# First attention of a decoder layer: queries rotated before the scores, both maps' scores as 64x64 quarters

## Chip, cores and metric

The kernel runs on one core of one Trainium2 chip. The metric is the device time of one launch in microseconds, as the median of several runs. The engines are TensorE (PE, with its weight loads shown apart as PEld), VectorE (DVE), ScalarE (ACT), GpSimd (POOL) and SyncE (SP), which here only issues DMAs. Each engine works through its own list of instructions in order, and semaphores order the lists against each other.

## What is computed

A decoder layer over 16 sequences of 128 tokens with 256 features: a first (differential) attention, a cross attention and a mixture of experts, each behind a layer norm and with a residual. The change touches the first attention alone:

```python
q = _apply_rope(q, cos, sin)            # 16 heads of 128; t*cos + rotate_half(t)*sin
k = _apply_rope(k, cos, sin)            # 4 key heads, each shared by 4 query heads
q1, q2 = (q[..., :64], q[..., 64:])
k1, k2 = (k[..., :64], k[..., 64:])
s1 = einsum('bhqd,bhkd->bhqk', q1, k1) / 8
s2 = einsum('bhqd,bhkd->bhqk', q2, k2) / 8
a1, a2 = softmax(masked s1), softmax(masked s2)     # causal, window of 64
diff = relu(a1 - lam * a2)
diff = diff / (sum(diff) + 1e-06)
out = (diff @ v) @ Wo
```

## The kernel before, in words

**Tiling.** The first attention runs in four groups `g` of four query heads with one key head. In a group there are 16 units `u`, one per sequence. Four units make a chunk `c` of 512 tokens. While the units of one chunk run, the projections of the next chunk are made: six items, `k`, `q0` to `q3` and `v`. `A_ITEMS` gives their order, `A_SLOT` the unit `j = u % 4` and the slot `s` at which each is made. They all go through the one PSUM bank `PJ`, so an item is projected only once the one before it has been taken out. The very first chunk is projected ahead of the loop, over four banks (`A_START`, `A_TURNS`). So 15 chunks are prepared inside units; the last four units prepare none.

**Order inside a unit.** Each engine's list is written out by hand in `a_unit`:
- PE: slot 0, the scores of unit `u` (L669), the transposes of `u-2` (L683, L685), slot 1, the product with the values of `u-2` (L692), the output projection of `u-3` (L701).
- DVE: denominators of `u-2` (L1100, L1105), residual of `u-4` (L1110), for `u-1` the reciprocal of the second map's sums and the ratio (L1080, L1084), **slot 0**, rho (L1088), the low part of the output of `u-3` (L1140), the difference of the maps of `u-1` (L1094), the row maxima of `u` (L1148, L1149), **slot 1**.
- ACT: slot 0 (the values' copy for item `v`), the copy of the transposes (`pt`, L1423), relu of `u-1` (L1500), the exponentials of `u` (L1456), slot 1, the copy `oah`, the mask written into the score banks for `u+2`.
- POOL: the normalisation of `u-2` (L1687), at `j = 0` the addition for the next chunk's keys (L1681), in the last chunk of a group the low parts of the next weights (L1675).

**Rotation.** In `a_take` DVE takes a query item out of PSUM with two multiplications of 128x512 (L1054): one product with (cos, -sin) for map 0, one with (sin, cos) for map 1, each over 128 rows. A key item costs three (L1044, L1046, the two of L1046 crossing between the halves of the partitions). POOL adds the key's two products, and four DMAs of 64 rows copy the rotated keys so that each map has its 64 key rows twice. The scores then contract over all 128 rows, and that contraction adds the two products of the query. One unit has 16 score products (2 maps, early and late query half, 4 heads), each with 64 columns of weights, so heads alternate between two column halves of the array. The trace shows each as two matmul records.

**Slots before.** `k` in (0, 1), `q0` in (1, 0), `q1` in (1, 1), `q2` in (2, 1), `v` in (3, 0), `q3` in (3, 1). On DVE, therefore, of the query and key items only `q0` stands in a slot 0.

Of the kernel before, what the change touches and what calls it, by code (L numbers as in the profile page):

```python
# [18 lines left out]
CB = 4  # L19
NC = B // CB  # L20
# [86 lines left out]
def decoder_kernel(nc, x, ctx_in, in_wqk, in_wv, in_wo, in_lam, in_taba, in_rawb, in_tabb, in_kvtab,  # L107
# [5 lines left out]
    def sem(name):  # L113
        return ctx.enter_context(nc.semaphore(name))
# [4 lines left out]
    with ctx:  # L119
# [111 lines left out]
        def quads(ap):  # L231
            return ap.rearrange("p (h k) -> p h k", k=S)
# [13 lines left out]
        a_hi, a_lo = sem("a_w_high"), sem("a_w_low")  # L246
        a_vf = sem("a_values_taken")
        a_pj, a_pf, a_k = sem("a_projected"), sem("a_projection_taken"), sem("a_k_ready")
        a_kd, a_tn = sem("a_k_copied"), sem("a_table_negated")
        a_sc, a_mx, a_ex = sem("a_scores"), sem("a_negmax"), sem("a_exp")  # L250
        a_mk = sem("a_mask_in_place")
        a_r2, a_rt, a_rh = sem("a_rec2"), sem("a_ratio"), sem("a_rho")
# [30 lines left out]

        A_ITEMS = ["k", "q0", "q1", "q2", "v", "q3"]
        AN, AV = len(A_ITEMS), A_ITEMS.index("v")
        A_SLOT = {(0, 1): 0, (1, 0): 1, (1, 1): 2, (2, 1): 3, (3, 0): 4, (3, 1): 5}
        AW = AN - 1


# [149 lines left out]
        def _(sp):  # L441
            for c in range(NC):
                if c == 0:
                    sp.dma_start(idf[:, :], ident).then_inc(s_const, 16)
                sp.dma_start(x_sb[:, CB * c:CB * (c + 1), :],
                             x[CB * c:CB * (c + 1)].rearrange("b p d -> p b d")).then_inc(s_x[c], 16)
                if c == 0:
                    sp.dma_start(raw_a[:, :, :], in_wqk[0]).then_inc(a_raw, 16)
                if c == 1:
                    sp.dma_start(taba[:, :, :], in_taba).then_inc(a_tab, 16)  # L450
                    for at in (0, QH):
                        sp.dma_start(maskf[at:at + QH, 0:QH], mask[0:QH, 0:QH]).then_inc(s_mask, 16)
                        sp.dma_start(masku[at:at + QH, :], mask[QH:S, :]).then_inc(s_mask, 16)
                    sp.dma_start(wv[:, :, :], in_wv).then_inc(a_wvl, 16)
            sp.dma_start(nlam[:, :], in_lam).then_inc(a_wld, 16)
            sp.dma_start(wo[:, :, :], in_wo).then_inc(a_wld, 16)
            for g in range(NG):
                if g < NG - 1:
                    sp.wait_ge(a_lo, g * AW + AW)
                    sp.dma_start(raw_a[:, :, :], in_wqk[g + 1]).then_inc(a_raw, 16)  # L460
                for c in range(NC):
                    sp.wait_ge(a_k, g * NC + c + 1)
                    for m in range(2):
                        for at in (0, 64):
                            sp.dma_start(kva[at:at + 64, c % 2, m, :], ktmp[64 * m:64 * m + 64, 0, :]).then_inc(a_kd, 16)
            sp.wait_ge(a_woh, NG)
            sp.wait_ge(a_wol, NG)
            sp.dma_start(raw_b[:, :], in_rawb[0]).then_inc(b_raw_s, 16)
# [78 lines left out]
        def _(pe):  # L547
# [69 lines left out]
            def a_unit(g, u, first=False, final=False, drain=False):  # L617
# [37 lines left out]
                if not drain:  # L655
                    if j == 0:
                        pe.wait_ge(a_pf, (g * NC + (c + 1)) * AW)
                        pe.wait_ge(a_vf, g * NC + (c + 1))
                        pe.wait_ge(a_kd, 64 * (g * NC + (c + 1)))
                    wait(pe, a_mk, n - 1)  # L660
                    tok = slice(S * j, S * (j + 1))
                    for m in range(2):
                        sc = A_S[u % 2][:, m, 0:SW]
                        if first and u < 2:
                            pe.matmul(sc, idb[:, :], maskb[:, :], start=True, stop=False, skip_group_check=True)
                        for at, to, keys in ((QH, late(sc), S), (0, early(sc), QH)):
                            for h in range(HG):
                                rows = slice(QH * (h % 2), QH * (h % 2) + QH)
                                last = pe.matmul(to[rows, h // 2, :],  # L669
                                                 qab[:, c % 2, m, h, S * j + at:S * j + at + QH],  # L670
                                                 kva[:, c % 2, m, S * j:S * j + keys],
                                                 start=False, stop=at == 0, skip_group_check=True)
                    last.then_inc(a_sc, 1)
                two = not (first and u < 2) and not (drain and u >= 2)
                if two:
# [219 lines left out]
            for c in range(len(A_START)):  # L895
# [4 lines left out]
                for item in A_START[c]:  # L900
                    if item == AV:
                        pe.wait_ge(a_wvl, 16)
                    a_project(0, 0, item, True, A_TURNS)
            pe.wait_ge(a_vf, 1)
            pe.wait_ge(s_cst, 3)
            pe.wait_ge(a_wld, 32)
            for u in range(UN):
# [79 lines left out]
        def _(dve):  # L987
# [47 lines left out]
            def a_take(g_to, c, item, turns=1):  # L1035

                chunk = g_to * NC + c
                if item == AV:
                    return
                dve.wait_ge(a_pj, chunk * AN + (item + 1))  # L1040
                src, par = quads(bank(PJ - (item % turns if turns > 1 else 0))), c % 2
                if item == 0:
                    wait(dve, a_kd, 64 * chunk)
                    dve.tensor_tensor(quads(ktmp[:, 0, :]), src, bcast(taba[:, 4, :]), ALU.mult)  # L1044
                    for to_, at in ((64, 0), (0, 64)):
                        last = dve.tensor_tensor(quads(ktmp[to_:to_ + 64, 1, :]), src[at:at + 64],  # L1046
                                                 taba[at:at + 64, 3, :].unsqueeze(1).broadcast_to([64, CB, S]),
                                                 ALU.mult)
                    last.then_inc(a_pf, 1)
                    return  # L1050
                h = a_tile(item) - 1
                to = ((qab[:, par, 0, h, :], 0), (qab[:, par, 1, h, :], 1))
                for dst, tab in to:
                    last = dve.tensor_tensor(quads(dst), src, bcast(taba[:, tab, :]), ALU.mult)  # L1054
                last.then_inc(a_pf, 1)

            def kv_step(i):
# [266 lines left out]
            ln_norm(0)  # L1324
            ln_stats(1)
            ln_low(0)
            dve.wait_ge(a_tab, 16)
            ln_norm(1)
            dve.wait_ge(s_const, 16)
            dve.wait_ge(s_mask, 64)  # L1330
# [1 line left out]
            dve.tensor_copy(early(maskb[:, :]), maskf[:, 0:QH].unsqueeze(1).broadcast_to([128, XP, QH]))\  # L1332
               .then_inc(s_cst, 1)
            dve.tensor_copy(late(maskb[:, :]), masku.unsqueeze(1).broadcast_to([128, XP, S])).then_inc(s_cst, 1)
            dve.tensor_scalar(taba[64:128, 0, :], taba[64:128, 0, :], -1.0, None, ALU.mult).then_inc(a_tn, 1)
            dve.tensor_scalar(taba[:, 3, :], taba[:, 3, :], -1.0, None, ALU.mult).then_inc(a_tn, 1)
            dve.wait_ge(a_tn, 2)
            for item in A_START[0]:
# [82 lines left out]
        def _(act):  # L1421
# [38 lines left out]
            def a_unit(g, u, first=False, final=False, drain=False):  # L1460
                n, c, j = g * UN + u, u // CB, u % CB

                def slot(s):
                    item = A_SLOT.get((j, s))
                    if item is None or drain or (final and c == NC - 1):
                        pass
                    elif item == AV:
                        a_take_v(g + 1 if c == NC - 1 else g, (c + 1) % NC)
                    elif c == NC - 2 and not final:
                        act.wait_ge(a_pj, (g * NC + (NC - 1)) * AN + (item + 1))  # L1470
                        a_high(g + 1, a_tile(item))
                    for what in A_EXTRA.get((a_part(first, final, drain), u, s), []):
                        if what[0] == "ln":
                            ln_take(what[1], what[2], PJ)
                        elif what[0] == "prep":
                            b_take(0, 0, what, what[1], None, bank(PJ))
                        elif what[0] == "kt2":
                            r = what[1]
                            act.wait_ge(b_kvp, r + 1)
                            if r == 0:  # L1480
                                act.wait_ge(a_sc, NG * UN - CB)
                            copy(kt2[:, CB * r:CB * (r + 1), :], quads(bank(PJ))).then_inc(b_kvc, 1)
                if u == 3 and not drain:
                    if first:
# [169 lines left out]
        def _(pool):  # L1654
# [23 lines left out]
            def a_keys(g_to, c):  # L1678

                pool.wait_ge(a_pf, (g_to * NC + c) * AW + 1)  # L1680
                pool.tensor_tensor(ktmp[:, 0, :], ktmp[:, 0, :], ktmp[:, 1, :], ALU.add).then_inc(a_k, 1)  # L1681

            def a_norm(n, par):

# [12 lines left out]
            def a_unit(g, u, first=False, final=False, drain=False):  # L1697
# [16 lines left out]
                    ln_rstd(6)  # L1714
                if drain:
                    return
                if final and c >= NC - 2:
                    if u == UN - 2 * CB:
                        a_keys(g, NC - 1)
                    return  # L1720
                if j == 0:
                    a_keys(g + 1 if c == NC - 1 else g, (c + 1) % NC)
                if 0 < u - CB * (NC - 2) <= CB:
                    for s in range(2):
                        item = A_SLOT.get(((u - 1) % CB, s), AV)
                        if item != AV:
                            a_low(g + 1, a_tile(item))
# [15 lines left out]
                a_low(0, tile)  # L1743
            a_keys(0, 0)
            ln_low(1)
            ln_rstd(2)
            ln_rstd(3)
            for u in range(UN):
# [211 lines left out]
```

## Time and profile before

| | us |
|---|---|
| median of 3 runs | 1334.43 (1333.85 to 1336.25) |
| the profiled execution | 1336.08 |
| its span in the trace | 1334.2 |
| busy PE / DVE / ACT / POOL | 1262.3 / 837.2 / 720.2 / 467.6 |
| mean granted PE clock | 0.986 of 2.4 GHz |

The first attention fills the span from about 28 to 480 us, the cross attention up to about 890, the experts the rest. A row of the trace has a start in us from the span's beginning, a duration, and in brackets the idle time just ahead of it with what ended it. Busy time tells how much an engine had to do, not who set the pace: for that one reads who waited for whom, unit by unit.

### The profile page before, as it was taken

The numbers are of one execution on the slowest core, as the hardware profiler recorded it, in microseconds if no ns is written. First come the engines' busy times: TensorE is split into PE (matmuls) and PEld (weight loads), VectorE is DVE, ScalarE is ACT, GpSimd is POOL, SyncE is SP. The second block draws the span as 40 slices with busy tenths as digits, with TensorE's granted clock in tenths as the row PEclk, the third lists the DMA queues.
The fourth block names the chain that finished last, engine by engine and source line by source line (L and its number), as shares of the span: only waits on it lengthen the run. The fifth ranks groups of instructions, "written<-read, shape, count | busy, mean of one in ns | idle before, by whom it ended". The sixth has DMA issues, their size and how long they took to land.

```text
span 1334.2 us, 27286 instructions
## 1 busy us (share of the span) xinstructions
PE 1262.3 (95%) x9584; PEld 993.9 (74%) x9584; DVE 837.2 (63%) x1986; ACT 720.2 (54%) x2746; POOL 467.6 (35%) x451
## 2 busy tenths in 40 slices
PE   5799999999999787999999999989999999999998
PEld 4678888888887564666666666657888888888887
DVE  6788888888888676566666656775443443434433
ACT  2788888888887753444444444464232332423322
POOL 3122113212211124445444544641152353533532
PEclk9899999999999989999999999999899999999999
DMA  6002000200012101111202101200324341144340
GB/s 222 17 18 57 18 17 18 57 17 17 17 34 92 31 16 48 60 33 58 67 17 92 33 17 33 76 1 1 111 67 139 68 126 52 39 139 77 57 93 31
DMA packets 34737, 72.78 MB, mean 55 GB/s; under 512 B 7872, under 2 KB 12992, under 8 KB 33344
## 3 DMA queue, kind: packets, MB, share of 16 engines
q1 hardware_dynamic: 34624, 71.32, 20.2%
q8 instruction: 66, 1.08, 0.3%
q14 instruction: 47, 0.39, 0.1%
HBM read 52.29 MB, written 2.23 MB: 41 GB/s over the span
## 4 chain that ended last, share of the span: by engine, by line
PE 74%; DVE 9%; ACT 8%; issue 4%; POOL 2%; DMA 1%; SPq 1%; DVEq 0%; POOLq 0%; ACTq 0%
PE ps L553 33%; PE ps L945 9%; PE ps L669 5%; PE ps L701 4%; PE ps L738 3%; PE ps L832 3%; ACT ea L1456 3%; PE ps L692 3%; PE ps L842 2%; PE ps L814 2%; PE ps L822 2%; PE ps L608 2%; ACT ea L1500 2%; DVE ea L1094 1%; PE ps L683 1%
## 5 line engine op out<-in xcount | busy, mean ns | idle before, releaser
L1828 POOL TENSOR_TENSOR sg<-sg,cw 128x512 f32<-128x512 f32 x88 | 113.6, 1291 | 260.4 <-ACT sg L1619 257.0
L1397 DVE TENSOR_TENSOR hh<-ps,sg 128x512 f32<-128x512 f32 x100 | 69.1, 691 | 179.1 <-POOL sg L1828 161.4
L1423 ACT ACTIVATE hhh<-hh 128x512 fp32r<-128x512 f32 x100 | 63.2, 632 | 213.8 <-DVE hh L1397 211.6
L1456 ACT ACTIVATE ea<-ps,negmax 128x64 f32<-128x64 f32 (+1 forms) x512 | 165.1, 342 | 6.7 <-DVE negmax L1149 6.7
L1423 ACT ACTIVATE pt<-ps 128x512 f32<-128x512 f32 x128 | 77.1, 602 | 169.7 <-PE ps L822 112.2
L1196 DVE TENSOR_TENSOR qcs<-ps,tabb 128x512 f32<-128x512 f32 x192 | 123.5, 686 | 64.8 <-PE ps L553 64.4
L553 PE MATMUL ps<-xnh,wch 128*128 128x512 f32 x400 | 157.3, 393 | 0.0
L553 PE MATMUL ps<-xnl,wch 128*128 128x512 f32 x400 | 157.1, 393 | 0.0
L553 PE MATMUL ps<-xnh,wcl 128*128 128x512 f32 x400 | 155.7, 389 | 0.0
L1687 POOL TENSOR_TENSOR ea<-ea,rden 128x128 f32<-128x128 f32 (+1 forms) x128 | 62.2, 506 | 263.1 <-DVE rden L1105 263.1
L1694 POOL TENSOR_TENSOR eb<-eb,rsum 128x512 f32<-128x512 f32 x64 | 67.4, 1054 | 180.2 <-DVE rsum L1240 180.0
L945 PE MATMUL ps<-wch,hhh 128*128 128x256 f32 x400 | 115.8, 290 | 4.2 <-DVE hhl L1399 2.4
L1399 DVE TENSOR_TENSOR hhl<-hh,hhh 128x512 fp32r<-128x512 f32 x100 | 75.5, 755 | 69.8 <-ACT hhh L1423 69.8
L945 PE MATMUL ps<-wch,hhl 128*128 128x256 f32 x400 | 113.6, 284 | 0.0
L945 PE MATMUL ps<-wcl,hhh 128*128 128x256 f32 x400 | 113.6, 284 | 0.0
L1456 ACT ACTIVATION_READ_ACCUMULATOR ea<-ps,negmax 128x1 f32 x512 | 107.3, 210 | 0.0
L1456 ACT ACTIVATE eb<-ps,negmax 128x128 f32<-128x128 f32 x256 | 90.7, 369 | 26.0 <-DVE negmax L1234 25.7
L669 PEld LDWEIGHTS ps<-kva,qab 128*64 128x64 f32 x2048 | 93.8, 140 | 13.2 <-issue 8.1
L669 PE MATMUL ps<-kva,qab 128*64 128x128 f32 (+1 forms) x2048 | 103.0, 254 | 0.0
L1619 ACT ACTIVATE sg<-ps 128x512 f32<-128x512 f32 x100 | 59.8, 598 | 71.9 <-PE ps L553 71.2
L701 PE MATMUL ps<-woh,oah 128*128 128x256 f32 x256 | 97.5, 381 | 0.7 <-DVE oal L1140 0.7
L1054 DVE TENSOR_TENSOR qab<-ps,taba 128x512 f32<-128x512 f32 x128 | 82.1, 683 | 19.5 <-PE ps L553 19.0
(154 smaller groups left out, 3307.3 us busy)
## 6 DMA issues: line engine op xcount, KB each, us to landing
raw_w<-in_rawb_dram SPq DMA_DIRECT2D x4, 2432.0 KB, 8.9
kva<-ktmp SPq DMA_DIRECT2D x64, 128.0 KB, 2.3
kvt<-qcs SPq DMA_DIRECT2D x64, 128.0 KB, 2.3
cw<-comb_d SPq DMA_DIRECT2D x32, 256.0 KB, 5.0
raw_w<-in_rawc_dram SPq DMA_DIRECT2D x4, 1920.0 KB, 8.4
cw<-comb_d SPq DMA_DIRECT2D x16, 224.0 KB, 4.8
raw_a<-in_wqk_dram SPq DMA_DIRECT2D x4, 768.0 KB, 5.8
cw<-comb_d SPq DMA_DIRECT2D x16, 192.0 KB, 5.8
```

Source lines behind the costliest of these rows:

```text
L553: last = pe.matmul(out_ap, w, m, start=n == 0, stop=n == len(steps) - 1)
L669: last = pe.matmul(to[rows, h // 2, :], qab[:, c % 2, m, h, S * j + at:S * j + at + QH], kva[:, c % 2, m, S * j:S * j + keys], start=False ...
L701: last = pe.matmul(ps[:, YB, 0:DM], o_[:, (u - 3) % 2, h, :], w_[:, h, :], start=h == 0 and i == 0, stop=h == HG - 1 and i == 2)
L945: last = pe.matmul(ps[:, j // 2, DM * (j % 2):DM * (j % 2 + 1)], h_[:, par, S * j:S * (j + 1)], w_[:, t, 2 * KT * 128:RC_T], start=begin a ...
L1054: last = dve.tensor_tensor(quads(dst), src, bcast(taba[:, tab, :]), ALU.mult)
L1196: last = dve.tensor_tensor(quads(qcs[:, b_at(t), m, :]), quads(bk), bcast(tabb[:, b_table(t), m, :]), ALU.mult)
L1397: dve.tensor_tensor(hh[:, par, :], bank(C_U[par]), sg[:, par, :], ALU.mult).then_inc(c_h, 1)
L1399: dve.tensor_tensor(hhl[:, par, :], hh[:, par, :], hhh[:, par, :].bitcast(f32), ALU.subtract)\
L1423: return act.activation(dst, src, ACT.Copy)
L1456: last = act.activation(dst(m, h), src, ACT.Exp, bias=negmax[:, par, i:i + 1], accum_out=sums[:, par, i:i + 1])
L1694: pool.tensor_tensor(src[:, par, :, :], src[:, par, :, :], rec[:, par, :].unsqueeze(2).broadcast_to([128, HG, S]), ALU.mult).then_inc(done, 1)
L1828: pool.tensor_tensor(sg[:, par, :], sg[:, par, :], cw[:, c % 2, t, :], ALU.mult).then_inc(c_hs, 1)
```

## The change

Queries are now rotated completely before the scores. DVE still makes two products per query item, one with cos in place and one with sin. SP sends the sine product across the two halves of the partitions with two DMAs of 64 rows into the other parity's buffer, and POOL adds it to the cosine product, one 128x512 addition per head (`a_queries`). The keys are added by POOL straight into `kva`; their four DMAs are gone. A map's score now contracts over 64 rows only: map 0 over partitions 0 to 63, map 1 over 64 to 127, so 16 products per unit run as 64x64 quarters, in an order that changes the quarter each time. The item order becomes `k, q0, q1, q2, q3, v`, in the slots (0, 0), (0, 1), (1, 0), (1, 1), (2, 0), (3, 0). For the first chunk DVE writes the sine products crossed by itself, in two halves per head. Table loads become four DMAs.

```diff
-        A_ITEMS = ["k", "q0", "q1", "q2", "v", "q3"]
+        A_ITEMS = ["k", "q0", "q1", "q2", "q3", "v"]
-        A_SLOT = {(0, 1): 0, (1, 0): 1, (1, 1): 2, (2, 1): 3, (3, 0): 4, (3, 1): 5}
+        A_SLOT = {(0, 0): 0, (0, 1): 1, (1, 0): 2, (1, 1): 3, (2, 0): 4, (3, 0): 5}
...
-                    sp.dma_start(taba[:, :, :], in_taba).then_inc(a_tab, 16)
+                    sp.dma_start(taba[0:64, :, :], in_taba[0:64]).then_inc(a_tab, 16)
+                    sp.dma_start(taba[64:128, 0, :], in_taba[64:128, 1]).then_inc(a_tab, 16)
+                    sp.dma_start(taba[64:128, 1, :], in_taba[64:128, 0]).then_inc(a_tab, 16)
+                    sp.dma_start(taba[64:128, 2:6, :], in_taba[64:128, 2:6]).then_inc(a_tab, 16)
...
-                    sp.wait_ge(a_k, g * NC + c + 1)
-                    for m in range(2):
-                        for at in (0, 64):
-                            sp.dma_start(kva[at:at + 64, c % 2, m, :], ktmp[64 * m:64 * m + 64, 0, :]).then_inc(a_kd, 16)
+                    for h in range(HG if g or c else 0):
+                        sp.wait_ge(a_pf, (g * NC + c) * AW + (h + 2))
+                        for to, at in ((64, 0), (0, 64)):
+                            sp.dma_start(qab[to:to + 64, 1 - c % 2, 1, h, :], qab[at:at + 64, c % 2, 1, h, :])\
+                              .then_inc(a_qx[h], 16)
...
-                        pe.wait_ge(a_kd, 64 * (g * NC + (c + 1)))
+                        pe.wait_ge(a_k, g * NC + (c + 1))
+                        pe.wait_ge(a_qr, HG * (g * NC + (c + 1)))
...
+                    for at, part, keys in ((QH, late, S), (0, early, QH)):
+                        for m, h in ((0, 0), (1, 1), (0, 1), (1, 0), (0, 2), (1, 3), (0, 3), (1, 2)):
+                            rows, d = slice(QH * (h % 2), QH * (h % 2) + QH), slice(64 * m, 64 * m + 64)
+                            last = pe.matmul(part(A_S[u % 2][:, m, 0:SW])[rows, h // 2, :],
+                                             qab[d, c % 2, 0, h, S * j + at:S * j + at + QH],
+                                             kva[d, c % 2, 0, S * j:S * j + keys],
+                                             start=False, stop=at == 0, skip_group_check=True)
...
-                to = ((qab[:, par, 0, h, :], 0), (qab[:, par, 1, h, :], 1))
-                for dst, tab in to:
-                    last = dve.tensor_tensor(quads(dst), src, bcast(taba[:, tab, :]), ALU.mult)
+                dve.tensor_tensor(quads(qab[:, par, 0, h, :]), src, bcast(taba[:, 0, :]), ALU.mult)
+                if turns == 1:
+                    last = dve.tensor_tensor(quads(qab[:, par, 1, h, :]), src, bcast(taba[:, 1, :]), ALU.mult)
+                else:
+                    for to_, at in ((64, 0), (0, 64)):
+                        last = dve.tensor_tensor(quads(qab[to_:to_ + 64, 1 - par, 1, h, :]), src[at:at + 64],
+                                                 taba[at:at + 64, 1, :].unsqueeze(1).broadcast_to([64, CB, S]),
+                                                 ALU.mult)
...
-                pool.tensor_tensor(ktmp[:, 0, :], ktmp[:, 0, :], ktmp[:, 1, :], ALU.add).then_inc(a_k, 1)
+                pool.tensor_tensor(kva[:, c % 2, 0, :], ktmp[:, 0, :], ktmp[:, 1, :], ALU.add).then_inc(a_k, 1)
+
+            def a_queries(g_to, c, heads):
+
+                for h in heads:
+                    if isinstance(g_to, int) and g_to == 0 and c == 0:
+                        pool.wait_ge(a_pf, h + 2)
+                    else:
+                        pool.wait_ge(a_qx[h], 32 * (g_to * NC + c))
+                    q = qab[:, c % 2, 0, h, :]
+                    pool.tensor_tensor(q, q, qab[:, 1 - c % 2, 1, h, :], ALU.add).then_inc(a_qr, 1)
+
+            A_TURNED = [(), (0,), (1, 2), (3,)]
...
                 if j == 0:
                     a_keys(g + 1 if c == NC - 1 else g, (c + 1) % NC)
+                a_queries(g + 1 if c == NC - 1 else g, (c + 1) % NC, A_TURNED[j])
...
             a_keys(0, 0)
             ln_low(1)
+            a_queries(0, 0, range(HG))
```

## Rows read from the trace of the kernel before

**Rows 1.** The page: busy time of each engine, share of the span.

```profile
PE 1262.3 (95%) x9584; PEld 993.9 (74%) x9584; DVE 837.2 (63%) x1986; ACT 720.2 (54%) x2746; POOL 467.6 (35%) x451
PE 74%; DVE 9%; ACT 8%; issue 4%; POOL 2%; DMA 1%; SPq 1%; DVEq 0%; POOLq 0%; ACTq 0%
```

**Rows 2.** Windows view, one chunk's four units: busy time of each engine.

```profile
299.23:326.08 26.85, 26.75 (x250) 22.21 (x249) 22.08 (x64) 23.42 (x113) 7.24 (x12) 1.00 0.09 21
```

**Rows 3.** Timeline of DVE in that chunk: start, duration, instruction.

```profile
299.23 0.18 DVE L1080 RECIPROCAL rec<-sums 128x4 f32<-128x4 f32 x1 [0.72 <-ACT ea L1456]
...
306.19 0.18 DVE L1080 RECIPROCAL rec<-sums 128x4 f32<-128x4 f32 x1 [0.19 <-ACT ea L1456]
...
307.29 0.99 DVE L1094 SCALAR_TENSOR_TENSOR ea<-ea,rho 128x64 f32<-128x64 f32 x4
...
309.13 0.68 DVE L1044 TENSOR_TENSOR ktmp<-ps,taba 128x512 f32<-128x512 f32 x1
309.82 1.39 DVE L1046 TENSOR_TENSOR ktmp<-ps,taba 64x512 f32<-64x512 f32 x2
...
312.09 0.18 DVE L1080 RECIPROCAL rec<-sums 128x4 f32<-128x4 f32 x1
...
312.96 1.29 DVE L1054 TENSOR_TENSOR qab<-ps,taba 128x512 f32<-128x512 f32 x2 [0.36 <-PE ps L553]
314.17 0.15 DVE L1088 TENSOR_TENSOR rho<-ratio,a_gap 128x4 f32<-128x4 f32 x1
...
319.65 0.18 DVE L1080 RECIPROCAL rec<-sums 128x4 f32<-128x4 f32 x1 [0.55 <-ACT ea L1456]
...
320.06 0.69 DVE L1088 TENSOR_TENSOR rho<-ratio,a_gap 128x4 f32<-128x4 f32 x1
```

**Rows 4.** Timeline of ACT in that chunk.

```profile
301.92 0.60 ACT L1423 ACTIVATE pt<-ps 128x512 f32<-128x512 f32 x1 [1.01 <-PE ps L685]
...
308.31 0.26 ACT L1500 ACTIVATE ea<-ea 128x64 f32<-128x64 f32 x1
...
309.39 0.30 ACT L1456 ACTIVATE ea<-ps,negmax 128x64 f32<-128x64 f32 x1
```

**Rows 5.** Chain that ended last, scores of a unit in either attention: start, time.

```profile
305.54 1.49 PE ps L669 x32
...
601.14 0.60 PE ps L814 x16
```

**Rows 6.** Timeline of POOL in that chunk.

```profile
311.29 1.29 POOL L1681 TENSOR_TENSOR ktmp<-ktmp 128x512 f32<-128x512 f32 x1 [5.37 <-DVE ktmp L1046]
...
319.25 1.48 POOL L1675 TENSOR_TENSOR wal<-raw_a,wah 128x256 fp32r<-128x256 f32 x2
```

**Rows 7.** Timeline of DVE at 422 us.

```profile
422.24 1.19 DVE L1094 SCALAR_TENSOR_TENSOR ea<-ea,rho 128x64 f32<-128x64 f32 x4
```

**Rows 8.** Timeline of POOL at 422 us.

```profile
421.65 0.97 POOL L1687 TENSOR_TENSOR ea<-ea,rden 128x128 f32<-128x128 f32 x2
```

**Rows 9.** Chain, crossing of the second attention's products: the later of four issues, then landing.

```profile
521.18 1.84 SPq L488
...
523.06 2.33 DMA kvt<-qcs
```

**Rows 10.** Timeline of PE: projections at full clock, then after an idle time.

```profile
312.07 0.40 PE L553 MATMUL ps<-xnh,wah 128*128 128x512 f32 x1
...
422.68 0.41 PE L683 MATMUL ps<-idf,ea 128*64 128x128 f32 x2 [2.17 <-POOL ea L1687]
...
423.66 0.63 PE L553 MATMUL ps<-xnl,wah 128*128 128x512 f32 x1
```

**Rows 11.** Chain: projection of the values of the first and the fourteenth prepared chunk.

```profile
54.55 1.80 PE ps L608 x16
...
404.14 1.79 PE ps L608 x16
```

**Rows 12.** Chain: the first unit's start.

```profile
29.14 0.32 PE ps L665
```

More of the change, by code:

```diff
@@ L248, in decoder_kernel @@
         a_pj, a_pf, a_k = sem("a_projected"), sem("a_projection_taken"), sem("a_k_ready")
-        a_kd, a_tn = sem("a_k_copied"), sem("a_table_negated")
+        a_qx = [sem(f"a_q_sines_crossed{h}") for h in range(HG)]
+        a_qr, a_tn = sem("a_q_rotated"), sem("a_table_negated")
         a_sc, a_mx, a_ex = sem("a_scores"), sem("a_negmax"), sem("a_exp")
@@ L658, in a_unit @@
                         pe.wait_ge(a_vf, g * NC + (c + 1))
-                        pe.wait_ge(a_kd, 64 * (g * NC + (c + 1)))
+                        pe.wait_ge(a_k, g * NC + (c + 1))
+                        pe.wait_ge(a_qr, HG * (g * NC + (c + 1)))
                     wait(pe, a_mk, n - 1)
                     tok = slice(S * j, S * (j + 1))
[L662 to L672, printed above, removed]
+                    if first and u < 2:
+                        for m in range(2):
+                            pe.matmul(A_S[u % 2][:, m, 0:SW], idb[:, :], maskb[:, :], start=True, stop=False,
+                                      skip_group_check=True)
+                    for at, part, keys in ((QH, late, S), (0, early, QH)):
[5 more added lines that the diff above has]
+                                             start=False, stop=at == 0, skip_group_check=True)
                     last.then_inc(a_sc, 1)
@@ L904, in _ @@
             pe.wait_ge(a_vf, 1)
+            pe.wait_ge(a_pf, AW)
             pe.wait_ge(s_cst, 3)
@@ L1042, in a_take @@
                 if item == 0:
-                    wait(dve, a_kd, 64 * chunk)
+                    wait(dve, a_k, chunk)
                     dve.tensor_tensor(quads(ktmp[:, 0, :]), src, bcast(taba[:, 4, :]), ALU.mult)
@@ L1326, in _ @@
             ln_low(0)
-            dve.wait_ge(a_tab, 16)
+            dve.wait_ge(a_tab, 64)
             ln_norm(1)
@@ L1334, in _ @@
             dve.tensor_copy(late(maskb[:, :]), masku.unsqueeze(1).broadcast_to([128, XP, S])).then_inc(s_cst, 1)
-            dve.tensor_scalar(taba[64:128, 0, :], taba[64:128, 0, :], -1.0, None, ALU.mult).then_inc(a_tn, 1)
+            dve.tensor_scalar(taba[64:128, 1, :], taba[64:128, 1, :], -1.0, None, ALU.mult).then_inc(a_tn, 1)
             dve.tensor_scalar(taba[:, 3, :], taba[:, 3, :], -1.0, None, ALU.mult).then_inc(a_tn, 1)
@@ L1480, in slot @@
                             if r == 0:
-                                act.wait_ge(a_sc, NG * UN - CB)
+                                act.wait_ge(a_sc, NG * UN - CB + 1)
                             copy(kt2[:, CB * r:CB * (r + 1), :], quads(bank(PJ))).then_inc(b_kvc, 1)
@@ L1716, in a_unit @@
                     return
-                if final and c >= NC - 2:
-                    if u == UN - 2 * CB:
-                        a_keys(g, NC - 1)
+                if final and c == NC - 1:
                     return
@@ L1722, in a_unit @@
                     a_keys(g + 1 if c == NC - 1 else g, (c + 1) % NC)
+                a_queries(g + 1 if c == NC - 1 else g, (c + 1) % NC, A_TURNED[j])
+                if final:
+                    return
                 if 0 < u - CB * (NC - 2) <= CB:
```

## Prediction

> **What bounds the kernel now.** The page comes first: PE is busy 95% of the span and makes up 74% of the chain that ended last [rows 1]. That invites the reading that every microsecond taken from PE is a microsecond won. The windows view of one chunk seems to agree: PE 26.75 of 26.85 us, ACT 23.4, DVE 22.1, POOL 7.2 [rows 2]. But a busy PE may be one that just keeps up, so I went on to the timelines of DVE and ACT in that chunk, and followed one closed loop through a unit. It starts when DVE takes the reciprocal of the second map's sums (L1080), which needs the exponentials of unit u-1. Then come ratio, whatever stands in slot 0, rho, the output's low part and the difference (L1094); then ACT's relu, which stands ahead of the exponentials in ACT's list; then the exponentials of unit u; then DVE's next L1080. In the unit that starts at 306.19, the difference begins 1.10 us after L1080 [rows 3], relu 2.12 us and the exponentials 3.20 us after it [rows 4], and the next L1080 stands at 312.09, 5.90 us later [rows 3]. PE has no part in this loop. DVE's rows in the same unit show the three key products, 2.08 us from 309.13 on, lying beside the exponentials, in slot 1, for nothing.
>
> The four windows from L1080 to L1080 are now readable. Unit j = 3, from 299.23: 6.96 us, because ACT's copy of the transposes waited 1.01 us for PE and relu stands behind it [rows 4]; this one is PE's. Unit j = 0: 5.90, the bare loop. Unit j = 1, from 312.09: 7.56; here `q0` stands in slot 0, DVE waited 0.36 us for its projection and needed 1.21 us from 312.96 to rho at 314.17. Unit j = 2, from 319.65: 6.43, the bare loop and 0.53 us in rho [rows 3], of which below. The sum is 26.85. So PE and the loop are both near the limit, but PE sets the time in one unit of four.
>
> **The change, part by part.**
>
> *Scores.* 32 records take 1.49 us per unit now. The nearest row for 64x64 quarters is the second attention's: 16 records in 0.60 us [rows 5], so 32 would take 1.20 us if each costs the same. Half of the records are only half as long, which gives at best 0.75 times this, 0.90 us. I take 1.05: 0.44 us less per unit, 1.8 us per chunk, 28 us over 64 units if PE were the bound. It isn't one afterwards (below), so what it buys is the PE wait of unit j = 3: its window goes from 6.96 to 5.90.
>
> *Slots.* DVE's work per item stays as it is: two products for a query, three for keys. But `k` moves from slot 1 to slot 0 of j = 0, `q1` takes the slot 0 of j = 1, where `q0` stood, and `q3` moves into slot 0 of j = 2. Slot 1 lies beside the exponentials, slot 0 lies in the loop. The windows become: j = 0, 5.90 + 2.08 = 7.98; j = 1, 5.90 + 1.21 = 7.11; j = 2, 7.11; j = 3, with `v` alone, which ACT takes out, 5.90. The sum is 28.1 us, 1.3 more than the 26.85 of before, although PE and DVE have no more to do than then. This is a floor: no part of the loop gets shorter.
>
> *POOL's additions.* `k` still costs one, and four queries are added: 4 x 1.29 us per chunk, by the same shape [rows 6]. POOL has the time (7.2 of 26.85 us busy), so as engine time they cost nothing. What they cost is DVE's. While a POOL operation runs, a DVE instruction that reads both inputs from SBUF does not start: rho, 0.15 us otherwise, took 0.69 from 320.06 to 320.75 [rows 3], just when POOL's 1.48 us from 319.25 ended [rows 6]; the difference at 422.24 took 1.19 in place of 0.99 [rows 7], POOL being busy till 422.62 [rows 8]. Products out of PSUM don't wait. The Trainium skill has this as a rule (page SBUF — State Buffer, section Who interferes with whom): a DVE instruction with two SBUF inputs and a GpSimd one that reads SBUF exclude each other, for the whole instruction. By that rule, the trace agrees, and without it this part would be free.
>
> Where do the additions fall? `k`: POOL starts when its products are done, at 2.5 us of window j = 0, and ends at 3.8. Rho slips in ahead, the 0.6 us low part reads PSUM, the difference would begin at 3.18 and waits till 3.86: 0.7 us. `q0`: its sine product is done at about 6.9 of window j = 0 (slot 1), the crossing costs two issues and a landing, bounded by the second attention's 1.84 + 2.33 = 4.2 us [rows 9] and by 1.2 + 2.33, so the addition starts at 1.7 to 2.4 of window j = 1, again against rho and the difference: 0.7. `q1`: its crossing is early, but POOL does the normalisation first (about 6.5 to 7.4), so the addition runs over the start of window j = 2 and holds ratio: 0.7. `q2` lands at 1.6 to 2.4 of window j = 2, right behind: 0.6. `q3` ends about with window j = 2, for nothing. Bounds of each: 0 and 1.29. I take 2.7 us per chunk, since each place follows from the order of the lists and not from chance: 30.8 us. The normalisation itself is not late, for it precedes the additions in POOL's list.
>
> *SP and DMA.* The wait for the key's copies goes; eight small DMAs per chunk come in place of four. The scores of the next chunk wait for `q3`'s addition, which ends before window j = 3 begins, one window ahead. The load of the second attention's first weights now stands behind the last crossing in SP's list, some two windows later than before, and is used only in the chunk after: no cost, or under 1 us once. DMA is busy 9% [rows 2].
>
> *Start.* The scores of unit 0 began at 29.14 [rows 12], behind `q3`'s products. Now DVE needs three products in place of two for each of four heads (2.7 us more), and POOL makes its four additions only behind its low part, the last some 1.3 us behind `q3`. The scores start about 3.4 us later; some of it returns, as `k` of the next chunk is then already projected. 2.5 us, between 0 and 4.
>
> *End.* The last four units prepare nothing and have shorter scores: 0 to 2 us gained, I take 2.
>
> **The sum.** Before, 14 prepared chunks are 13 intervals from 54.55 to 404.14 [rows 11], 26.9 us each. Afterwards 30.8: 3.9 more for 13 chunks, 50.7. The first two run beside layer norms, which fill part of DVE's list there already: 2.5 more each (between 1.3 and 3.9), 5. With the start 2.5 and the end -2: 56 us. The profiled execution took 1336.1 us for a span of 1334.2; it becomes 1392. The median of before is 1.7 us lower, so I forecast **1390 us**. PE then has about 24.3 us of work in 30.8.
>
> The Trainium skill (page TensorEngine Tiling (Array Packing), section PSUM Bottleneck) warns that after a TensorE speed-up by tiling, the emptying of PSUM may become the bottleneck. The rows say it already is half of the bound here: the loop consists of DVE and ACT instructions alone.
>
> **The rivals.**
>
> *A, the forecast:* the loop carries two more items and the additions. 1390. Chance 0.60.
>
> *B, the additions find gaps.* If most of them start beside instructions that read PSUM, the chunk is 28.1 to 29: 15 x 1.3 to 15 x 2.1 is 20 to 32 us, 1355 to 1366. For it: the row maxima, the products and the low part read PSUM and together fill over a third of a window. Against it: the places worked out above. 0.17.
>
> *C, the clock falls too.* With the loop as bound PE idles. At the start of window j = 3 it has done everything up to the transposes and waits for ACT's copy, by my count up to 3 us. Before, after 2.17 us idle, projections took 0.63 us in place of 0.40 [rows 10]: the 1.2 GHz level in place of 2.4. Then the output projection and `k`'s projection behind it take 1.3 us longer, and DVE waits for `k` at the slot 0 of j = 0. At up to 1.3 us for most chunks: 8 to 20 us on A, 1398 to 1410. 0.15.
>
> *D, PE was the bound (faster).* If slot 0's items found room in waits of DVE that I took for loop, the 0.44 us per unit come back: 1334 - 27 is 1307, with the start 1310. This decides if the bare loop is under 5.90 - 0.8 us, so that 4 windows with 4.5 us of items fit into 25 us. Rows 3 and 4 show no idle time of that size in it. 0.06.
>
> *E, the quarters don't overlap.* If products in different quarters run no faster than now, PE has 26.1 us of work per chunk, still under 28.1: the time is A's or B's. As a case of its own with no change in time: 0.02.
>
> **How the numbers follow.** The range takes in B's low end and most of C: 1354 to 1405. A measurement of this kernel can tell about 0.2%, 2.7 us, from no change. Faster by more 0.06, within 0.02, slower 0.92.
>
> **What would show it.** DVE's rows per chunk: windows of about 8.7, 7.8, 8.4 and 5.9 us; L1044 and its followers between ratio and rho; rho or difference lengthened, each ending with a POOL addition. ACT waiting for DVE's difference as its largest wait. PE busy about 80% in 160 to 480 us and waiting for DVE's takes. 32 score records in 0.9 to 1.2 us. The second attention and the experts as long as before. I am wrong if the chunk comes below 28 us, if windows with an item in slot 0 are 5.9 us, or if rho and difference keep their durations next to POOL's additions.

## Result and profile after

The changed kernel takes **1400.65 us** (median of 4 runs, 1396.79 to 1409.33), the kernel before 1334.3 us (1333.85 to 1336.25): slower by 5.0%, ratio 1.050 with a 95% interval of 1.0477 to 1.0524. The forecast was 1390, range 1354 to 1405. The profiled execution took 1396.8 us with a span of 1395.0, so the traces have 60.8 us between them to explain.

The page of the changed kernel: busy time, then the chain by engine, then ACT's relu and POOL's query additions (busy, mean ns, idle before and what ended it).

```profile
PE 1249.3 (90%) x9584; PEld 956.7 (69%) x9584; DVE 867.2 (62%) x1990; ACT 721.3 (52%) x2746; POOL 550.3 (39%) x515
PE 58%; DVE 17%; ACT 15%; issue 7%; POOL 2%; DMA 1%; SPq 0%; DVEq 0%; POOLq 0%; ACTq 0%
...
L1512 ACT ACTIVATE ea<-ea 128x64 f32<-128x64 f32 (+1 forms) x256 | 69.2, 273 | 96.5 <-DVE ea L1106 96.5
L1703 POOL TENSOR_TENSOR qab<-qab 128x512 f32<-128x512 f32 x64 | 83.2, 1303 | 36.5 <-DMA qab<-qab 36.5
```

Beside [rows 1] PE has fallen from 74% to 58% of the chain, DVE has gone from 9 to 17 and ACT from 8 to 15. POOL's 64 query additions are new, 83.2 us. Ahead of its relu (now L1512) ACT stood idle for 96.5 us waiting for DVE's difference (now L1106), before for 19.1: that is the loop, seen from ACT.

One undisturbed chunk, windows view (time, then busy PE, PEld, DVE, ACT, POOL, granted clock, DMA share, GB/s), to be put beside [rows 2]:

```profile
256.00:286.26 30.26, 24.58 (x246) 18.98 (x238) 23.50 (x63) 22.52 (x110) 10.29 (x13) 1.00 0.16 36
```

PE now works 24.6 of 30.3 us, at full clock. Timeline of DVE in that chunk, lines that answer to [rows 3]: L1092 (was L1080) opens each window, L1096 is the ratio, L1100 rho, L1106 the difference, L1051 and L1053 take the keys, L1059 and L1061 a query.

```profile
256.00 0.18 DVE L1092 RECIPROCAL rec<-sums 128x4 f32<-128x4 f32 x1 [1.08 <-ACT ea L1468]
...
256.40 0.69 DVE L1051 TENSOR_TENSOR ktmp<-ps,taba 128x512 f32<-128x512 f32 x1
257.11 1.39 DVE L1053 TENSOR_TENSOR ktmp<-ps,taba 64x512 f32<-64x512 f32 x2
258.53 0.16 DVE L1100 TENSOR_TENSOR rho<-ratio,a_gap 128x4 f32<-128x4 f32 x1
...
259.34 1.34 DVE L1106 SCALAR_TENSOR_TENSOR ea<-ea,rho 128x64 f32<-128x64 f32 x4
...
264.49 0.18 DVE L1092 RECIPROCAL rec<-sums 128x4 f32<-128x4 f32 x1 [1.09 <-ACT ea L1468]
...
266.68 2.03 DVE L1106 SCALAR_TENSOR_TENSOR ea<-ea,rho 128x64 f32<-128x64 f32 x4
...
272.51 0.18 DVE L1092 RECIPROCAL rec<-sums 128x4 f32<-128x4 f32 x1 [1.09 <-ACT ea L1468]
272.73 0.69 DVE L1096 TENSOR_TENSOR ratio<-rec,sums 128x4 f32<-128x4 f32 x1
...
274.54 0.50 DVE L1100 TENSOR_TENSOR rho<-ratio,a_gap 128x4 f32<-128x4 f32 x1
...
280.36 0.18 DVE L1092 RECIPROCAL rec<-sums 128x4 f32<-128x4 f32 x1 [1.59 <-ACT ea L1468]
...
286.26 0.18 DVE L1092 RECIPROCAL rec<-sums 128x4 f32<-128x4 f32 x1 [0.67 <-ACT ea L1468]
```

The windows are 8.49, 8.02, 7.85 and 5.90 us. The last one, with nothing of DVE's in slot 0, is the bare loop of before to a hundredth. And POOL in the same stretch, to be laid beside DVE's lengthened lines:

```profile
258.58 1.29 POOL L1693 TENSOR_TENSOR kva<-ktmp 128x512 f32<-128x512 f32 x1 [3.72 <-DVE ktmp L1053]
...
266.73 1.37 POOL L1703 TENSOR_TENSOR qab<-qab 128x512 f32<-128x512 f32 x1 [2.59 <-DMA qab<-qab]
...
272.12 1.28 POOL L1703 TENSOR_TENSOR qab<-qab 128x512 f32<-128x512 f32 x1
273.75 1.27 POOL L1703 TENSOR_TENSOR qab<-qab 128x512 f32<-128x512 f32 x1 [0.35 <-DMA qab<-qab]
```

Each addition holds up a VectorE instruction with two inputs in SBUF (this exclusion is "the port" below): POOL's 258.58 to 259.87 meets the difference at 259.34 (1.34 in place of 1.00); 266.73 to 268.10 meets it at 266.68 (2.03); the ratio at 272.73 ends at 273.42, with the addition that ended at 273.40; rho at 274.54 ends at 275.04, with the one from 273.75 on, which ended at 275.02.

**Where the 60.8 us are.** Counting from L1080 or L1092 of one chunk to that of the next:

| stretch | before | after | difference |
|---|---|---|---|
| first L1080/L1092 at | 39.89 | 42.02 | 2.1 |
| first 13 chunks | 351.9 | 407.0 | 55.1 (4.24 each) |
| next two | 66.1 | 69.7 | 3.6 |
| last units, nothing prepared | 28.2 | 25.9 | -2.3 |
| second attention, experts | | | 2.3 |

The undisturbed chunk gives 3.9 (30.26 against 26.4 in the best chunks of before). Most of the rest of the 4.24 is in window j = 3 of three chunks, one in each group behind the first: 7.02, 6.77 and 6.78 us instead of 5.90. There ACT converts the group's output weights (1.09 us) just ahead of the values and the copy of the transposes. Before, that window was PE's, 6.99 with this conversion against 6.96 without, so the conversion cost nothing; now it costs 0.9 to 1.1.

### The profile page after: what moved, and what is told of

Same layout as the page of the kernel before. It is cut to its first block, busy times and chain, and to the rows that moved or that the text cites. A ratio compares the mean times of both kernels' runs of the same rounds, so it can differ in the third digit from the quotient of the medians.

```text
span 1395.0 us, 27420 instructions
## 1 busy us (share of the span) xinstructions
PE 1249.3 (90%) x9584; PEld 956.7 (69%) x9584; DVE 867.2 (62%) x1990; ACT 721.3 (52%) x2746; POOL 550.3 (39%) x515
## 4 chain that ended last, share of the span: by engine, by line
PE 58%; DVE 17%; ACT 15%; issue 7%; POOL 2%; DMA 1%; SPq 0%; DVEq 0%; POOLq 0%; ACTq 0%
PE ps L558 27%; PE ps L952 9%; ACT ea L1468 8%; DVE ea L1106 4%; ACT ea L1512 3%; PE ps L744 3%; PE ps L838 3%; PE ps L848 2%; PE ps L820 2%; PE ps L828 2%; PE ps L707 2%; PE ps L698 2%; DVE ktmp L1053 2%; DVE qab L1061 1%; DVE rho L1100 1%
## 5 line engine op out<-in xcount | busy, mean ns | idle before, releaser
L1512 ACT ACTIVATE ea<-ea 128x64 f32<-128x64 f32 (+1 forms) x256 | 69.2, 273 | 96.5 <-DVE ea L1106 96.5
L698 PE MATMUL ps<-pt,kva 128*128 128x512 f32 x128 | 74.8, 668 | 42.3 <-DVE oal L1152 24.6
L558 PE MATMUL ps<-xnh,wah 128*128 128x512 f32 x160 | 71.1, 445 | 41.2 <-DVE qab L1061 21.7
L707 PE MATMUL ps<-woh,oah 128*128 128x256 f32 x256 | 100.7, 393 | 0.7 <-DVE oal L1152 0.7
L1703 POOL TENSOR_TENSOR qab<-qab 128x512 f32<-128x512 f32 x64 | 83.2, 1303 | 36.5 <-DMA qab<-qab 36.5
```

The lines of the kernel that those rows point to most:

```text
L558: last = pe.matmul(out_ap, w, m, start=n == 0, stop=n == len(steps) - 1)
L698: pe.matmul(bank(OB), quads(kva[:, (w // CB) % 2, 2, :])[:, w % CB, :], pt[:, u % 2, :, :], start=True, stop=True).then_inc(a_pv, 1)
L707: last = pe.matmul(ps[:, YB, 0:DM], o_[:, (u - 3) % 2, h, :], w_[:, h, :], start=h == 0 and i == 0, stop=h == HG - 1 and i == 2)
L1512: last = act.activation(e, e, ACT.Relu, accum_out=rsum[:, par, h:h + 1])
L1703: pool.tensor_tensor(q, q, qab[:, 1 - c % 2, 1, h, :], ALU.add).then_inc(a_qr, 1)
```

## Experiments

The kernel before was run beside each; its median lay between 1334.3 and 1336.1.

**Old scores, new slots.** The kernel before with the item order and slots alone:

```diff
-        A_ITEMS = ["k", "q0", "q1", "q2", "v", "q3"]
+        A_ITEMS = ["k", "q0", "q1", "q2", "q3", "v"]
-        A_SLOT = {(0, 1): 0, (1, 0): 1, (1, 1): 2, (2, 1): 3, (3, 0): 4, (3, 1): 5}
+        A_SLOT = {(0, 0): 0, (0, 1): 1, (1, 0): 2, (1, 1): 3, (2, 0): 4, (3, 0): 5}
...
+            pe.wait_ge(a_pf, AW)
...
-                                act.wait_ge(a_sc, NG * UN - CB)
+                                act.wait_ge(a_sc, NG * UN - CB + 1)
```

The two waits, one ahead of the first unit and one at the change to the second attention, go with the new order.

> The kernel before with nothing changed but the item order and the slots of the change (k in slot 0 of j = 0, q3 in slot 0 of j = 2): no query additions, no crossing, old scores. Theory (slots): DVE's windows 8.0 to 8.7, 7.1, 7.1 and 5.9 to 6.9; chunk 28.2 to 29.5 in place of 26.9: 1334 + 15 x 1.3 to 2.6 = 1354 to 1373 us. Rival A (PE is the bound, its work is the same): 1334 +- 4. Rival B (only additions and crossings made the change slow): 1334 +- 4.

Measured: 1375.2 us (ratio 1.030, 1.0277 to 1.0324), 39 us more, with the same work on every engine. That is just over the expected range, and both rivals fall. Its DVE timeline, one chunk (L1081 opens a window, L1095 is the difference):

```profile
309.29 0.18 DVE L1081 RECIPROCAL rec<-sums 128x4 f32<-128x4 f32 x1 [1.08 <-ACT ea L1457]
...
316.28 0.18 DVE L1081 RECIPROCAL rec<-sums 128x4 f32<-128x4 f32 x1 [0.79 <-ACT ea L1457]
...
323.27 0.18 DVE L1081 RECIPROCAL rec<-sums 128x4 f32<-128x4 f32 x1 [1.10 <-ACT ea L1457]
...
329.83 0.18 DVE L1081 RECIPROCAL rec<-sums 128x4 f32<-128x4 f32 x1 [0.59 <-ACT ea L1457]
...
333.23 1.34 DVE L1095 SCALAR_TENSOR_TENSOR ea<-ea,rho 128x64 f32<-128x64 f32 x4
...
338.37 0.18 DVE L1081 RECIPROCAL rec<-sums 128x4 f32<-128x4 f32 x1 [1.08 <-ACT ea L1457]
```

6.99, 6.99, 6.56, 8.54, together 29.1: a query in slot 0 costs 1.09 us (I had 1.21), the keys 2.3 plus 0.35 for POOL's addition. In the 6.56 ACT's copy of the transposes still waited 0.63 us for PE, which the long scores cause.

**The additions away.** The changed kernel with the four query additions over 4 columns:

```diff
-                    q = qab[:, c % 2, 0, h, :]
-                    pool.tensor_tensor(q, q, qab[:, 1 - c % 2, 1, h, :], ALU.add).then_inc(a_qr, 1)
+                    q = qab[:, c % 2, 0, h, 0:4]
+                    pool.tensor_tensor(q, q, qab[:, 1 - c % 2, 1, h, 0:4], ALU.add).then_inc(a_qr, 1)
```

> The changed kernel with POOL's four query additions per chunk made over 4 columns in place of 512; that part of the rotation is left out, all waits and DMAs stay. Theory (loop plus port): the additions cost by holding off DVE's two-input instructions. Windows from 8.5, 8.0, 7.9, 5.9 to about 8.5, 7.1, 7.1, 5.9; 1.7 us less for each of 15 chunks: 1396.8 - 26 = 1371 us, 1365 to 1376. Rival (the moved slots alone made the kernel slower, the additions are free): 1395 to 1405 as before the edit.

Measured: 1374.6 us (1.029, 1.0257 to 1.0316), 26 us less than the changed kernel, as expected. An undisturbed chunk has windows 6.99, 6.99, 5.90, 8.48: 28.36 in place of 30.26. In it all differences have 1.00 us again, but the one behind the keys, 1.34.

**The additions moved.** Nothing left out; POOL only waits for the unit's difference first, so that the additions run beside DVE's instructions that read PSUM:

```diff
+                wait(pool, a_df, n)
                 if j == 0:
                     a_keys(g + 1 if c == NC - 1 else g, (c + 1) % NC)
                 a_queries(g + 1 if c == NC - 1 else g, (c + 1) % NC, A_TURNED[j])
```

> The changed kernel, where POOL waits for the difference of the unit (L1106) before its key and query additions, so that they run beside DVE's maxima and products out of PSUM. Nothing is left out. Theory (port): windows 8.0, 7.1, 7.1, 5.9 = 28.1; about 2.1 us less for each of 15 chunks, 31 us: 1366, 1360 to 1372. Rival 1 (the port costs nothing, POOL's time or the crossing does): no change or slower than 1397. Rival 2 (a new wait: POOL's normalisation of the next unit comes late behind the additions and PE's transposes with it): windows shrink less, 1375 to 1390.

Measured: 1369.7 us (1.026, 1.0242 to 1.0278), 31 us less than the changed kernel for one added wait. Its DVE timeline, and one of POOL's additions with the two DVE instructions that now ran beside it:

```profile
307.17 0.18 DVE L1092 RECIPROCAL rec<-sums 128x4 f32<-128x4 f32 x1 [1.09 <-ACT ea L1468]
309.36 1.00 DVE L1106 SCALAR_TENSOR_TENSOR ea<-ea,rho 128x64 f32<-128x64 f32 x4
...
310.52 1.28 POOL L1703 TENSOR_TENSOR qab<-qab 128x512 f32<-128x512 f32 x1 [3.70 <-DVE ea L1106]
310.60 0.68 DVE L1161 TENSOR_REDUCE negmax<-ps 128x4 f32<-128x512 f32 x1
311.20 0.68 DVE L1059 TENSOR_TENSOR qab<-ps,taba 128x512 f32<-128x512 f32 x1
...
314.17 0.18 DVE L1092 RECIPROCAL rec<-sums 128x4 f32<-128x4 f32 x1 [0.92 <-ACT ea L1468]
...
321.16 0.18 DVE L1092 RECIPROCAL rec<-sums 128x4 f32<-128x4 f32 x1 [1.59 <-ACT ea L1468]
...
327.07 0.18 DVE L1092 RECIPROCAL rec<-sums 128x4 f32<-128x4 f32 x1 [0.67 <-ACT ea L1468]
330.39 1.00 DVE L1106 SCALAR_TENSOR_TENSOR ea<-ea,rho 128x64 f32<-128x64 f32 x4
...
335.20 0.18 DVE L1092 RECIPROCAL rec<-sums 128x4 f32<-128x4 f32 x1 [1.09 <-ACT ea L1468]
```

7.00, 6.99, 5.91, 8.13: 28.03, where the prediction had put 28.1 for the slots without the port. It does better than the additions nearly left out, since the keys' addition has moved too. So the additions cost nothing as POOL's work or as a wait for their result; they cost by their place.

**Half the scores.** The kernel before with half of its score products left out (`for h in range(2)` in place of `range(HG)` around L669).

> The kernel before with half of its score products left out (heads 2 and 3 of each group get none), all other work the same: PE has 0.75 us less per unit, 48 us in all. Theory (PE sets only one window in four): window j = 3 goes from 6.96 to 5.9 and DVE's 0.36 us wait at j = 1 goes; 1.1 to 1.4 us per chunk, 16 to 21 us: 1313 to 1318. Rival (PE busy 99% is the bound): 1286 to 1292.

Measured: 1325.5 us (0.992, 0.9906 to 0.9942), 10.6 less. The scores of a unit took 0.82 us in place of 1.49, so PE had 43 us less to do (not the 48 I had reckoned), and a quarter of that arrived: less than even my theory had. The windows 7.56, 5.90, 6.96, 5.90 of before became 7.56, 5.89, 6.11, 5.90 (j = 1, 2, 3, 0). Window j = 3 gave back 0.85; the wait at j = 1 did not go, because what it waits for is not PE's pace: `q0` can be projected only when DVE has taken `k` out of the one bank. PE's timeline in this kernel shows PE itself waiting for that; its projection then takes 1.67 us, and DVE starts at 307.10:

```profile
305.40 0.50 PE L553 MATMUL ps<-xnh,wah 128*128 128x512 f32 x1 [0.50 <-DVE ktmp L1046]
```

The changed kernel's scores take as long as these (0.83 us). In the slots of before, therefore, quicker scores were worth some 10 us and no more.

**The quarters.** The changed kernel, with two products in one quarter before the next:

```diff
-                        for m, h in ((0, 0), (1, 1), (0, 1), (1, 0), (0, 2), (1, 3), (0, 3), (1, 2)):
+                        for m, h in ((0, 0), (0, 2), (0, 1), (0, 3), (1, 0), (1, 2), (1, 1), (1, 3)):
```

> The changed kernel with its 16 score products per unit in an order that stays in one quarter of the array for two products before it goes on, instead of changing it each time. Nothing is left out. Theory (DVE and ACT are the bound, PE has some 6 us to spare per chunk): the 32 score records go from 0.83 us to 1.2 to 1.7 us, the time stays within 5 us of the changed kernel's 1397 to 1409. Rival (PE's shorter scores still carry time): slower by 0.4 to 0.9 us x 64 = 25 to 55 us.

Measured: 1403.6 us (1398.35 to 1407.2), the changed kernel's time, as expected of a PE that isn't the bound. But the premise was a miss: a unit's scores took 0.89 us on the chain in place of 0.83, not 1.2 to 1.7. This order is nearly as good; the experiment didn't make the scores expensive, so it tests little.

**Better slots.** Four versions of the changed kernel that take DVE's items out of slot 0. First, the slots of before, with `v` last and all query additions in the units j = 2 and j = 3:

```diff
-        A_SLOT = {(0, 0): 0, (0, 1): 1, (1, 0): 2, (1, 1): 3, (2, 0): 4, (3, 0): 5}
+        A_SLOT = {(0, 1): 0, (1, 0): 1, (1, 1): 2, (2, 1): 3, (3, 0): 4, (3, 1): 5}
-            A_TURNED = [(), (0,), (1, 2), (3,)]
+            A_TURNED = [(), (), (0, 1), (2, 3)]
```

> The changed kernel with the slots of before: k (0, 1), q0 (1, 0), q1 (1, 1), q2 (2, 1), q3 (3, 0), v (3, 1); POOL adds q0 and q1 at j = 2, q2 and q3 at j = 3. Theory (slots plus port): windows 5.9, 7.0, 5.9, 7.0 = 25.8 plus 1 to 2.5 us from the additions, 26.8 to 28.3 per chunk: 1337 to 1360 us. Rival (the additions and crossings are the main cost): 1380 or more. Rival (PE would set the pace again): windows with nothing in slot 0 above 6.5.

Measured: 1379.2 us (1.032, 1.0292 to 1.0349). A miss, 19 us above the range. The windows of one chunk were 7.6, 7.1, 8.0 and 7.9 for j = 1, 2, 3, 0. The 7.6 has the 0.36 us wait for `q0` that I had left out. Two of them hold the additions, as foreseen (differences of 1.71 and 2.02 us). The 7.9 at j = 0 I had not seen coming; it stands in five of the first 14 chunks (7.7 to 8.2), the others have 5.9 to 6.5 there. With `v` in slot 1 of j = 3 ACT copies it only after its exponentials, and the scores of the next chunk wait for it. Timeline of PE in this kernel:

```profile
277.21 1.11 PE L675 MATMUL ps<-kva,qab 64*64 64x128 f32 x32 [2.58 <-ACT kva L1435]
...
279.55 0.63 PE L558 MATMUL ps<-xnl,wah 128*128 128x512 f32 x1
```

After 2.58 us idle, PE comes back at the 1.2 GHz level (0.63 us for a projection, as in [rows 10], and a granted clock of 0.50 from 279.5 to 281 us), `k` is projected late, and DVE, which waited 1.38 us for it, takes it only at 281.64, 5 us into the window.

Second, the keys last, which need no crossing, so that only `q1` stands in slot 0 (the weights' tiles are mapped to the new order; shown is the core):

```diff
-        A_ITEMS = ["k", "q0", "q1", "q2", "q3", "v"]
+        A_ITEMS = ["q0", "q1", "q2", "q3", "v", "k"]
-        A_SLOT = {(0, 0): 0, (0, 1): 1, (1, 0): 2, (1, 1): 3, (2, 0): 4, (3, 0): 5}
+        A_SLOT = {(0, 1): 0, (1, 0): 1, (1, 1): 2, (2, 1): 3, (3, 0): 4, (3, 1): 5}
...
+                if j == CB - 1:
+                    a_keys(g + 1 if c == NC - 1 else g, (c + 1) % NC)
```

> The changed kernel with the items in the order q0, q1, q2, q3, v, k in the slots of before, so that only q1 stands in a DVE slot 0 and the keys, which need no crossing, come last. POOL adds q0 at j = 1, q1 at j = 2, q2, q3 and the keys at j = 3. Theory: windows 5.9, 7.0, 5.9, 5.9 = 24.7, plus up to 3.2 us from five additions wherever they fall: 26.0 to 27.9 per chunk, 1324 to 1352 us.

Measured: 1366.4 us (1.023, 1.0205 to 1.0252), 14 above the range, its chunks 27.8 to 31.1 us behind the first two. The shortest had 8.55, 6.43, 6.43 and 6.43: the wait for `q1`'s projection, and an addition's delay in every window. Third, the same with the additions behind the difference:

> The kernel of the run before (keys last), and POOL waits for the unit's difference before its additions. Theory: windows 5.9, 7.0, 5.9, 5.9 = 24.7 plus 0.2 for the keys' addition and 0.4 for the normalisation behind it, 25.2 to 25.6 per chunk against 26.9 before: 1334 - 15 x 1.5 + 2 = 1313 us, 1308 to 1322, faster than both kernels. Rival (PE, with 24.1 us of work in 25.3, becomes the bound again, its gaps cost): 1320 to 1335. Rival (shortening the loop brings nothing since PE was the bound): 1334 or more.

Measured: 1340.4 us (1.004, 1.0027 to 1.0052). The added wait brings 26 us again, but the whole is no faster than before; the expected 1313 is missed. Windows of an undisturbed chunk were 7.47, 5.89, 6.30, 6.52, together 26.18. Its windows view:

```profile
292.50:318.68 26.18, 24.48 (x248) 19.28 (x247) 21.70 (x63) 22.32 (x110) 10.18 (x13) 1.00 0.18 41
```

7.47 has the wait for `q1`'s projection that I had left out although [rows 3] show its like; 6.30 has one of 0.40 us for the keys' projection, behind which their three products no longer fit beside the exponentials; and 6.52 is the keys' addition, which ends 0.6 us into the window and holds back the scores and, in POOL's list, the normalisation. Chunks with the conversion of the output weights have 27.0 to 27.2, those with the low parts of the next weights 27.5 to 28.8 (before, 26.9). The time falls where my second rival had put it (1334 or more), but not for its reason: PE worked 24.48 of the 26.18 us, and the window with nothing added is 5.89. What the shorter loop met instead are waits between DVE and PE through the one bank PJ, and POOL's place behind the keys.

The last version has the keys in slot 1 of j = 0 and two queries in slot 0, the additions behind the difference:

```diff
-        A_SLOT = {(0, 0): 0, (0, 1): 1, (1, 0): 2, (1, 1): 3, (2, 0): 4, (3, 0): 5}
+        A_SLOT = {(0, 1): 0, (1, 0): 1, (1, 1): 2, (2, 0): 3, (2, 1): 4, (3, 0): 5}
-            A_TURNED = [(), (0,), (1, 2), (3,)]
+            A_TURNED = [(), (), (0, 1), (2, 3)]
...
+                if A_TURNED[j]:
+                    wait(pool, a_df, n)
```

> The changed kernel with k back in slot 1 of j = 0 and q0 (1, 0), q1 (1, 1), q2 (2, 0), q3 (2, 1), v (3, 0); POOL adds q0 and q1 at j = 2, q2 and q3 at j = 3, each time only after the unit's difference. Two items stand in a DVE slot 0, 1.06 us each by the runs so far. Theory: windows 5.9, 7.0, 7.0, 5.9 = 25.8, 25.8 to 26.5 per chunk against 26.4 to 26.9 before, start and second chunk 2 to 4 us slower: 1326 to 1338 us, so even with the kernel before. Rival (PE's 24.1 us per chunk with its waits carry the time as with the keys last): 1338 to 1345.

Measured: 1345.9 us (1.008, 1.0068 to 1.0094), a miss by 8, and 1 above its rival's 1345: windows 7.56, 7.00, 6.11, 5.90. The 7.56 is that of before, with the same wait for `q0` behind `k`.

**The port in the kernel before.** POOL's low parts of the next weights wait for the difference (one `wait(pool, a_df, n)` ahead of `a_low`).

> The kernel before, where POOL's low parts of the next group's weights wait for the unit's difference, so that they no longer hold off rho. Nothing else is changed. Theory (port): the 0.53 us in rho go twice in each of three groups, and PE takes part of it back at j = 3: 1 to 3 us less, 1331 to 1334 us. Rival (the port costs nothing there): no change.

Measured: 1334.0 against 1335.4 us, ratio 0.9994 (0.9984 to 1.0004): no change that can be told. In the trace the windows of 6.4 at j = 2 became 6.2 in three chunks, under 1 us in all. Rho is back at 0.16 us; part of what it gave back goes into a wait of 0.22 us for ACT's `oah`. The mechanism is there, its price is too small here.

## Why the prediction came out right

*The bound.* Right, and the centre of it. With its work shortened by 43 us in the kernel before, PE gave back 10.6; with its work unchanged and only the slots moved, the kernel lost 39. A PE busy 95% of the span was not the bound, but stood close behind a loop of DVE and ACT.

*Scores.* I took 1.05 us per unit between 0.90 and 1.20; the chain shows 0.83 for 32 records. Under my lower end, and without effect on the time.

*Slots.* 28.1 us per chunk were forecast for the slots alone, 28.03 measured with the port cleared. Inside it a query is smaller than its rows (1.09, not 1.21), since it begins sooner in the window, 0.31 us after its start where the forecast had 0.41, and the keys a little larger (2.2, not 2.08).

*Port.* Forecast 2.7 us per chunk (0.7, 0.7, 1.3 and 0), measured 30.26 - 28.03 = 2.2: the keys' 0.35, `q0`'s 1.03, `q1`'s and `q2`'s together 0.86, `q3`'s none. The places were right but for `q2`'s, which began 1.24 us into window j = 2 where I had 1.6 to 2.4. The keys' cost half of the 0.7 I had reckoned: the difference began at 259.34, 0.53 us before the end of the addition at 259.87, and took 0.35 us longer. `q0`'s landed 2.24 us into its window, in the bound of 1.7 to 2.4, in the middle of the difference. Over the chunks it came at 1.2 to 2.9: at 1.2, in chunks before 210 us, it held rho (up to 1.07 us), mostly with windows of 7.8 to 7.9; at 2.2 to 2.8 it held the difference (2.0 us), with windows of 8.0; and at 2.9, in one chunk, it came behind the difference and cost nothing (6.97). Where it lands can matter more: in the profile of the kernel with the other order of quarters it came at 2.37 in a chunk with two low-part operations of POOL right behind it, and the difference took 3.05 us. In the changed kernel's profile it came at 2.75 in the same chunk, and the difference took 2.02.

```profile
235.97 3.05 DVE L1106 SCALAR_TENSOR_TENSOR ea<-ea,rho 128x64 f32<-128x64 f32 x4
```

That such landings vary from run to run could be why the changed kernel's runs spread over 12.5 us and those before over 2.4. The spread of the other versions doesn't settle it (7 us with additions over 4 columns, 3.3 with additions behind the difference), and I have not tested it.

*What was missing.* The forecast was 10.7 us short, about 5 of it in the profiled span (60.8 against 56). There larger misses cancel. The first two prepared chunks cost 3.5 and 4.4, where I had 2.5 each: 2.9 too little. The next eleven cost 4.3 each, where I had 3.9: 4.3 too little, of which about 3 is ACT's conversion of the output weights, in three windows j = 3, free as long as PE was late there, on the path once it was not. The prediction named what hides PE's wait but didn't ask what else that wait had hidden. The last two cost 3.6 together, where I had 7.8: 4.2 too much. About 2 us lie in later stages, for which I had nothing. The rest of the 10.7 is in the medians: that of the changed kernel is 3.9 above its profiled execution, where before it was 1.8 below.

*Luck.* The 30.8 us that I gave every chunk is close to the mean of those eleven, 30.94, but not by its terms: the undisturbed chunk has 30.26, and those with converted weights 31.2 to 31.6. That the port was taken too dear and the weights were left out gave nearly the right mean.

*The rivals.* B (gaps in the port): the experiment with the moved additions comes near its time, 1369.7 against 1355 to 1366, and shows that it takes an extra wait to get there. C (clock): the mean granted clock is 0.92 in 52 to 160 us, where it was 0.99 before, and 1.00 in the undisturbed chunk; it happens early and not in most chunks. I had counted up to 3 us of idle time at j = 3. There is less, since the values' projection, the scores and the transposes come just ahead of that wait. PE's timeline in the changed kernel's undisturbed chunk:

```profile
282.57 1.12 PE L698 MATMUL ps<-pt,kva 128*128 128x512 f32 x2 [1.10 <-ACT pt L1435]
```

PE waited 1.10 us there, and 1.85 at 275.78, the longest wait in this chunk; the clock held through both. What the lower clock of 52 to 160 us cost, no run separates. D (the bound is PE's work) fell with the old scores in new slots and with half the scores. E was not the case: the scores took 0.83 us in place of 1.49.

## To carry to other kernels

A busy share near 100% doesn't make an engine the bound: look for the closed loop of waits through all engines, give it its length in time from an undisturbed unit, and see which of an engine's instructions stand inside the loop and which beside it. Moving the same work from beside to inside cost 39 us here, more than halving the score products of the busiest engine brought. When an engine's work gets shorter, ask what its lateness used to hide, and place GpSimd's work by what VectorE reads at that moment.

## What the runs showed of the hardware

- A GpSimd operation on SBUF operands and a VectorE instruction with both inputs in SBUF held each other up: rho, 0.16 us otherwise, took up to 1.07, and a row of four VectorE instructions, 0.99 us alone, took 1.34 beside the end of one addition, 2.03 with a whole one inside it and 3.05 with one and two low-part operations behind it. The addition inside such a row took 1.37 us in place of 1.28. VectorE's products and reductions out of PSUM ran beside GpSimd at their usual 0.68 us. One wait that moved five additions beside these was worth 31 us.
- Sixteen fp32 products in 64x64 quarters, half of them 128 and half 64 columns long, took 0.83 us, against 1.49 us for the sixteen of the kernel before, of the same lengths, in 128x64 halves. Two in a row in one quarter cost 0.06 us more in all.
- After 2.58 us idle the 1.2 GHz level was back on TensorE (a projection in 0.63 us, 0.40 otherwise).
